# Reordering the first stage of a fused four-layer kernel: lower products one cycle later, upper weights turned at once, another place for the rotary side jobs

## What is computed

```python
# per batch e of 4: x[e] is 512 x 512, guw = fside_sq[e] (512 x 512), dw = ctx[e] (512 x 256)
def smooth_quant_linear(x, w):
    s = sqrt(max(amax(|x|, axis=0), EPS) / max(amax(|w|, axis=0), EPS))     # one factor a column
    xs, ws = x / s, w * s
    x_scale, w_scale = rowmax(|xs|) / 127, rowmax(|ws|) / 127
    return round(xs / x_scale) @ round(ws / w_scale).T * x_scale * w_scale.T

def expert(xe, guw, dw):
    gate, up = split(smooth_quant_linear(xe, guw), 2)                       # the "upper" linear
    return smooth_quant_linear(silu(gate) * up, dw)                         # the "lower" linear

x = x + tanh(g_xattn[0]) * expert(layernorm(x), fside_sq, ctx)              # layer 1: this stage
x = x + tanh(g_ffn[0])   * moe(layernorm(x), ...)
x = x + tanh(g_xattn[1]) * attention(layernorm(x), ctx, rotary positions, ...)
x = x + tanh(g_ffn[1])   * moe(layernorm(x), ...)
```

## Time and profile before

| | us |
|---|---|
| three runs, median | 1309.74 |
| lowest, highest | 1307.85, 1311.29 |
| profiled execution | 1311.2 |
| its span | 1309.5 |
| first stage: last write to X | 217.85 from the span's start |
| next stage: first transfer issued | 222.35 |

### The profile page before, as it was taken

One profiled execution on the slowest core, in us unless ns is written; L12 is line 12 of the kernel. 1 busy time (PEld: TensorE's weight loads), 2 busy tenths in 40 slices (PEclk: granted clock), 3 DMA queues, 4 the chain that ended last, 5 costly groups with the idle time before them and its releaser, 6 DMA issues.

```text
span 1309.5 us, 16528 instructions
## 1 busy us (share of the span) xinstructions
PE 1169.4 (89%) x5292; PEld 508.2 (39%) x5293; DVE 831.5 (63%) x1292; ACT 661.6 (51%) x1157; POOL 398.6 (30%) x465
## 2 busy tenths in 40 slices
PE   5877776998999999968889989999999999889997
PEld 4554442555444444423222223222322222234543
DVE  6788665335455554155878888778877777724543
ACT  2665564465222222244466666566656656763453
POOL 4456541102322222042234432222222233102332
PEclk8988898999999999988999999999999999999999
DMA  7334124654544444188314443222222225300011
GB/s 244 126 105 137 49 97 159 226 211 161 192 146 156 149 148 135 54 255 196 90 48 139 128 126 94 79 77 83 75 82 82 79 81 61 50 1 9 33 41 49
DMA packets 111893, 145.79 MB, mean 111 GB/s; under 512 B 25048, under 2 KB 79832, under 8 KB 111560
## 3 DMA queue, kind: packets, MB, share of 16 engines
q1 hardware_dynamic: 92680, 113.47, 27.2%
q0 software_dynamic: 18368, 28.85, 8.6%
q10 hardware_dynamic: 768, 2.49, 0.6%
HBM read 99.54 MB, written 48.37 MB: 113 GB/s over the span
## 4 chain that ended last, share of the span: by engine, by line
PE 33%; DVE 10%; issue 7%; ACT 5%; POOL 1%; DMA 1%; ACTq 0%; POOLq 0%; DVEq 0%
PE PS L2902 7%; PE PS L2803 5%; PE PS L2868 5%; PE PS L2887 4%; DVE a_top L3263 4%; PE PS L2827 3%; PE PS L2387 2%; ACT shared_w L3023 2%; ACT a_E L3023 2%; PE PS L2410 1%; PE PS L1980 1%; PE PS L2014 1%; POOL a_K L2147 1%; DMA a_rows<-f_y,l_pos 1%; PE PS L2815 0%
## 5 line engine op out<-in xcount | busy, mean ns | idle before, releaser
L3263 DVE TENSOR_REDUCE a_top<-PS 128x2 f32<-128x1024 f32 x256 | 309.3, 1222 | 88.4 <-PE PS L2887 84.9
L2868 PE MATMUL PS<-a_Q,a_K 99*128 99x512 bf16 (+1 forms) x512 | 166.2, 386 | 15.1 <-ACT a_E L3023 3.2
L3023 ACT ACTIVATE shared_w<-PS 128x512 f32<-128x512 f32 x256 | 138.8, 596 | 74.7 <-PE PS L2868 74.6
L3023 ACT ACTIVATE a_E<-PS 128x512 f32<-128x512 f32 x256 | 138.9, 596 | 63.7 <-PE PS L2868 63.5
L1498 PE MATMUL PS<-f_W,f_GT 128*128 x312 | 142.2, 599 | 0.2 <-ACT f_GT L1532 0.2
L2887 PE MATMUL PS<-a_K,a_Q 64*128 64x512 bf16 x512 | 100.5, 390 | 7.9 <-DVE a_top L3263 6.4
L1927 POOL TENSOR_TENSOR a_qf<-a_qf,a_tab 128x512 f32<-128x512 f32 x15 | 19.1, 1270 | 286.4 <-DVE a_swapped L3165 286.4
L2868 PEld LDWEIGHTS PS<-a_Q,a_K 99*128 99x128 bf16 (+1 forms) x512 | 44.1, 97 | 150.1 <-ACT a_E L3023 51.1
L1554 DVE TENSOR_TENSOR f_H<-f_SG,PS 128x256 f32<-128x256 f32 x39 | 16.4, 421 | 115.5 <-ACT f_SG L1538 115.5
L1498 PEld LDWEIGHTS PS<-f_W,f_GT 128*128 128x128 f32 x312 | 56.9, 192 | 57.9 <-issue 57.9
L2803 PE MATMUL PS<-a_xT,a_early 128*128 128x512 f32 x128 | 72.9, 667 | 2.0 <-ACT a_xT L2989 0.7
(11 more groups left out here) (382 smaller groups left out, 2076.8 us busy)
## 6 DMA issues: line engine op xcount, KB each, us to landing
f0r_raw<-in_L_ffn_W_dram SPq DMA_DIRECT2D x24, 512.0 KB, 5.3
a_K<-k_parts SPq DMA_DIRECT2D x192, 64.0 KB, 2.3
a_Q<-a_q_parts SPq DMA_DIRECT2D x186, 64.0 KB, 2.4
f_y<-f_Y SPq DMA_DIRECT2D x39, 256.0 KB, 2.0
v_units<-V SPq DMA_DIRECT2D x16, 512.0 KB, 2.9
a_V<-v_units SPq DMA_DIRECT2D x16, 512.0 KB, 3.6
k_parts<-f_k_parts SPq DMA_DIRECT2D x16, 384.0 KB, 3.4
a_q_parts<-a_parts SPq DMA_DIRECT2D x16, 384.0 KB, 2.8
```

Source lines behind the costliest of these rows:

```text
L2868: nc.tensor.matmul(PS[:, 4 + h % 2, :], K6[k][0:rows_, o, head // 2, kt * P:(kt + 1) * P], Q6[k][0:rows_, o, head // 2, :], start=True, st ...
L3023: nc.scalar.activation(E[step % 2][:, h, :], PS[:, 4 + h % 2, :], ACT.Exp).then_inc(exp_done, 1)
L3263: nc.vector.tensor_reduce(top[:, h - h % 2:h - h % 2 + 2, t], PS[:, 2 * pair:2 * pair + 2, :], AX.X, ALU.max).then_inc(maxed, 1)
```

## The change

The order on all four engines is rewritten; no arithmetic is changed. In cycle i there is now a third batch, `e = i - 2`: its lower products and their rescaling (y) go into the front of cycle i, in banks 4, 5, 6 and again 4, and POOL adds y of batch b - 2 in its pass b. PE turns the first half of the upper weights as soon as they are shifted and no longer behind the lower wsc_row; the upper products come before the turn of the lower xs. DVE has `gate` behind `s_columns(up)`, and the lower reductions later. ACT loads the root's table right behind silu (by `norm_root`, or by a spare Sqrt, `bring_root`), and makes the waves of batch i at the end of cycle i, ahead of slot 7; r of batches 1 to 3 stands in slot 7 of the cycle before, now in front of the slot's own job. The numbers of jobs in the slots stay.

```diff
-        DOWN_AT = (4, 5, 6, 0)
+        DOWN_AT = {b: (4, 5, 6, 4) for b in range(NB - 2)}
+        DOWN_AT[NB - 2] = (4, 5, 6, 2)
+        DOWN_AT[NB - 1] = (0, 1, 2, 5)
@@ POOL
             for b in range(NB):
                 side.pool_angles(pool, b)
-                if b:
-                    (adds y of batch b - 1)
+                if b >= 2:
+                    add_batch(b - 2)
+                if b == NB - 1:
+                    add_batch(NB - 2)
                 side.pool_tables(pool, b)
@@ PE, cycle i
                 turn_w(up, u, 1, 2)
-                if d >= 0: turn_w(down, d, 0, 4)
                 turn_w(up, u, 0, 0)
...
                 turn_x(up, u, 0, 0)
+                if e >= 0:
+                    pe.wait_ge(down.xqT_ready, e + 1)
+                    lower_products(e, (0, 1, 2))
                 side.tensor(pe, i, 1)
-                if d >= 0: turn_down_x(d)
+                if e >= 0:
+                    pe.wait_ge(y_ready, e * TB + 1)
+                    lower_products(e, (3,))
                 s_rows(up, u, (0, 0), (1, 0))
+                if d >= 0: turn_w(down, d, 0, 4)          # waits for y of batch e
                 side.tensor(pe, i, 2)
-                if d >= 0: s_rows(down, d, (6, 0), (6, 256))
+                if d >= 0: turn_down_x(d, 4)
                 side.tensor(pe, i, 3)
                 wsc_row(up, u, 1)
                 side.tensor(pe, i, 4)
+                pe.wait_ge(up.w_shifted, u + 1)
+                turn_shifted(up.ws, 0, (2, 3), up.wqT_done)
+                if d >= 0: s_rows(down, d, (6, 0), (6, 256))
                 side.tensor(pe, i, 5)
-                if d >= 0: wsc_row(down, d, 4)
-                finish_up(u)
-                side.tensor(pe, i, 6)
-                if d >= 0: finish_down(d)
+                (the rest of what finish_up was)
+                if d >= 0:
+                    wsc_row(down, d, 4)
+                    turn_down_ws(d)
                 pe.wait_ge(up.xqT_ready, 2 * u + 2)
                 for t in range(TB):
                     product(up, t, t)
-                if d >= 0: (lower products 0 to 2)
+                side.tensor(pe, i, 6)
+                if d >= 0: turn_down_xs(d)
                 side.tensor(pe, i, 7)
-                if d >= 0: (lower product 3)
@@ ACT, cycle i
                 if d >= 0:
-                    side.scalar(act, d, 7)
-                    side.scalar_waves(act, d)
                     silu(d)
+                    if u < NB - 1: norm_root(u + 1)
+                    else: bring_root()
                 side.scalar(act, i, 0)
-                side.scalar(act, i, 1)
                 root(up, u)
-                if d >= 0:
-                    root(down, d)
-                    if u < NB - 1: norm_root(u + 1)
+                side.scalar(act, i, 1)
...
                 take_wsc_row(up, u, 1)
+                if d >= 0: root(down, d)
                 side.scalar(act, i, 4)
+                take_up_w(u, 0, 2)
                 shift_x(up, u)
...
+                take_up_w(u, 1, 0)
                 side.scalar(act, i, 5)
-                take_up_w(u)
                 if d >= 0:
                     shift_w(down, d)
                     take_wsc_row(down, d, 4)
-                    shift_x(down, d)
+                if 0 < u < NB - 1: normalize(u + 1)
+                if d >= 0:
+                    take_down_w(d)
+                    shift_x(down, d)
                 side.scalar(act, i, 6)
-                if d >= 0: take_down_w(d)
+                if u == 0: normalize(1)
+                if u < NB - 1:
+                    side.scalar_waves(act, u)
+                    side.scalar(act, i, 7)
                 if d >= 0: take_down_x(d)
-                if u < NB - 1: normalize(u + 1)
@@ ACT, tail
             d = NB - 1
+            silu(d)
+            bring_root()
             side.scalar(act, d, 7)
-            silu(d)
@@ DVE, cycle i: new order
+                reduce_turned(up) x4; ratio(up)
+                if e >= 0: take_down(e, (0, 1))
+                s_columns(up)
+                if e >= 0: take_down(e, (2,))
+                if u == 1: row_stats(3)
+                if d >= 0: gate(d)
+                if e >= 0: take_down(e, (3,))
+                scale_w(up); reduce_turned(down, d, 0); w_scales(up)
+                reduce_turned(down, d, 1); ratio(down)
+                scale_x(up); s_columns(down); x_scales(up); row_shifts(u + 1)
+                scale_w(down); w_scales(down); take_up_x(u)
+                scale_x(down); x_scales(down); gate_scale(d); take_up(u)
@@ SideJobs
-    ANGLES = 1
+    ANGLES = ((0, 1), (0, 7), (1, 7), (2, 7))
-                slots.append(flat[:many] + ([(i, "r", 0)] if s == self.ANGLES and i < self.NB else []))
+                slots.append([(b, "r", 0) for b in range(self.NB) if self.ANGLES[b] == (i, s)] + flat[:many])
```

More of the change, by code:

```diff
@@ L448, in normalize, with bring_root @@
                 last.then_inc(up.x_ready, 1)
+            def bring_root():
+                nc.scalar.activation(spare_root[:], ln_eps[:], ACT.Sqrt)
             norm_root(0)
@@ L602, in gate_scale, with take_down @@
                 ch.wait()
-            def take_down(b, last):
+            def take_down(b, tiles):
                 v.wait_ge(down.wsc_row_ready, b + 1)
@@ L607, in take_down @@
                     v.wait_ge(x_updated, b * TB)
-                for t in range(TB):
+                for t in tiles:
                     v.wait_ge(down.product_done, b * TB + t + 1)
-                    nc.vector.scalar_tensor_tensor(y[:, t, :], PS[:, (LAST_AT if last else DOWN_AT)[t], :], gated_scale[:, t:t + 1], down.wsc_row[:],
+                    nc.vector.scalar_tensor_tensor(y[:, t, :], PS[:, DOWN_AT[b][t], :], gated_scale[:, t:t + 1], down.wsc_row[:],
                                                    ALU.mult, ALU.mult).then_inc(y_ready, 1)
-                    if last and t:
-                        add_rows(b, t - 1)
-                if last:
-                    add_rows(b, TB - 1)
             def add_rows(b, t):
@@ L633, in _ @@
                 reduce_turned(up, u, 3, 0)
+                ratio(up, u)
+                if e >= 0:
+                    take_down(e, (0, 1))
+                s_columns(up, u)
+                if e >= 0:
+                    take_down(e, (2,))
+                if u == 1:
+                    row_stats(3)
                 if d >= 0:
                     gate(d)
-                ratio(up, u)
-                s_columns(up, u)
+                if e >= 0:
+                    take_down(e, (3,))
+                scale_w(up, u, 1, 0)
+                if d >= 0:
+                    reduce_turned(down, d, 0, 4)
+                w_scales(up, u)
                 if d >= 0:
@@ L640, in _ @@
                     ratio(down, d)
-                scale_w(up, u, 1, 0)
+                scale_x(up, u, 0, 0)
                 if d >= 0:
                     s_columns(down, d)
-                w_scales(up, u)
-                x_scales(up, u, 0, 0)
+                x_scales(up, u)
+                if 0 < u < NB - 1:
+                    row_shifts(u + 1)
                 if d >= 0:
@@ L649, in _ @@
                     w_scales(down, d)
-                    x_scales(down, d, 6, 0)
+                if u == 0:
+                    v.wait_ge(x_loaded[1], 16)
+                    row_stats(1)
+                take_up_x(u)
+                if u == 0:
+                    row_shifts(1)
+                if d >= 0:
+                    scale_x(down, d, 6, 0)
+                    x_scales(down, d)
                     if d == 0:
@@ L677, in _ @@
             w_scales(down, d)
-            x_scales(down, d, 6, 0)
+            scale_x(down, d, 6, 0)
+            x_scales(down, d)
             gate_scale(d)
-            take_down(d, True)
+            for t in range(TB):
+                take_down(d, (t,))
+                if t:
+                    add_rows(d, t - 1)
+            add_rows(d, TB - 1)
             v.wait_ge(x_updated, NB * TB)
```

145 lines of the change are left out of this document (63 added, 82 removed).

## The result

| | before | after |
|---|---|---|
| median of the runs, us | 1309.72 (with the runs made beside the kernel after) | 1326.19 (1325.49 to 1327.38) |
| span of the profiled execution | 1309.5 | 1324.7 |
| last write to X in the first stage | 217.85 | 230.42 |
| rest of the span | 1091.65 | 1094.3 |

What follows compares the result with a forecast made beforehand. DVE carries most of the first stage's chain, with holes for the root, hs and turned weights. A1 54.35, cycles 46.1 and 43.4, last cycle and tail 77.2 end it at 221.05 (+3.2): 1312.9 us, range 1303.5 to 1319.

Steps and rivals of the forecast that it cites:

- the new middle: Upper x_scaled to upper products, with ACT as the chain: 7.0 us, where it took 13.3 and 15.0 before.
- A1: End of the pass over batch 0, when PE starts turning batch 1's upper weights: 54.35, against 50.06 before.
- signs of being wrong: Gate at 1.4, small steps at 0.17, PE's side job behind ang at 1.9 each time, or A1 below 52.
- The new end of a cycle: Upper products to PE's next turn of upper weights, behind the wait for ang: 10.9 in cycle 1, 8.55 in cycle 2.
- the clock's 0.8: PE's side job after the wait for ang may run at the low clock: half of 1.7, 0.8 in cycle 1.
- the rival that it falls each time: PE's clock drops after every wait for ang: another 3.1 us, 1316.0; slower, by this or larger stalls, had 0.37.
- The front, with stalls beside POOL: Start of upper weight turns to x_scaled on DVE, stalls of 3.5 included: 27.4 in cycle 1, 27.0 in cycle 2.
- part 3: DVE's work from the start of upper weight turns to x_scaled, without stalls: 23.5 us, against 25.4 before.
- Last cycle, from the products on: Last upper products to stage end, V job behind silu and root table; last cycle and tail 77.2 against 75.3.
- Edits at nothing: add_batch on POOL, stores on SP's queue, the split of x_scales and spare_root (0.2) were taken to cost nothing.
- DVE runs through: Rival: small steps fall into POOL's gaps and PE's clock stays high: -6.2 us, 1303.6; chance 0.21.
- the even exchange: Rival: cycle ends give back what the middle gains, 1309.7; chance 0.42 together with no change and the forecast.

Runs made afterwards that it cites:

- tail_copies: Kernel after, with ACT in the tail copying slot 7's two V jobs before silu(3) and the root's table: ratio 1.0066 to the kernel before.
- no_angles_after: Kernel after, with POOL's reduction of the angles left out (rotary tables hold other numbers): ratio 1.0063 to the kernel before.
- own_jobs_later: Kernel after, with the jobs behind r in slot 7 of cycles 0 to 2 moved to slot 0 of the next cycle: ratio 1.0033 to the kernel before.
- tail_gate_first: r_own_tail, with gate ahead of every y in the tail: ratio 0.9897 to the kernel before, 1295.76 us.
- r_own_tail: Kernel after, with r back in its own cycle and, in the tail, ACT's slot 7 copies ahead of silu(3): ratio 0.9906 to the kernel before.

## Why the prediction was wrong, point by point

Against the forecast the end of the stage came 9.4 us late (230.42 for 221.05).

Three steps failed, all of them terms of the sum that were too small: the stalls beside POOL in the front of the cycles, gate above all (+7.3), the new middle (+3.5), and the part from the last upper products on, where gate stands beside POOL's additions (+3.9). A1 and the cycle ends, forecast too long, took back 5.4. Two of the forecast's own signs of being wrong came, A1 below 52 and a side job behind ang at about 1.9; both hang on the execution that was profiled, as the next lines tell.

- **A1** (forecast 54.35, measured 50.90, -3.4). The products ran 2.5 earlier than summed, of which 1.9 is the early turn of x in the first pass and not the change. The step itself, V job behind ang behind waves, came as told: PE's wait was 3.57, I had 3.8. With x turned late, the same code up to there gave 54.97 in tail_copies, so that the -3.4 is mostly the luck of this execution, in the forecast's favour: it hid a part of the miss.
- **The new end of a cycle**, from the products to the next A: 10.65 and 8.53. The working (10.9 and 8.55) was right to 0.3; the clock's 0.8 on top wasn't there, as the side jobs of four matmuls behind ang took 1.98 each. In tail_copies, with the same code, they took 3.64 and 2.50, in no_angles_after 1.98 and 3.40. So the level goes either way from one execution to the next, which is what a half of 1.7 meant; the rival that it falls each time is out.

```profile
51.49 3.64 PE L1851 MATMUL PS<-wkv,cT 128*128 128x512 f32 x4 [3.57 <-ACT ang L1871]
```

- **The new middle** (7.0): 7.8, 8.4 and 8.3, so +3.5 in three cycles. The step was mis-sized. PE waited 1.11, 0.77 and 0.77 for ACT's copy of the lower row in front of the lower turns, which stand ahead of the products, and in cycle 1 a side job at the clock's low level (3.62, at 77.84) ran into the chain.
- **The front, with stalls beside POOL** (27.4, 27.0, 27.0): 28.6, 29.1 and 31.0, +7.3 in all. This is the largest miss. I put 1.1 on gate, the size of one stall; it had 1.5, 2.6 and 2.4, which is 3.2 of the 7.3. Each of gate's four instructions can be held up, and I counted one. The small steps lost 8.3 in the three cycles where I had 7.2. The waits for copies and turned tiles inside the front, and the first turns of the last cycle at the clock's low level (3.09 for 1.91), are most of the rest. About 0.8 is an error of addition: the terms of part 3 add up to 23.85 and not 23.5, and with row_stats(3) in place of the y's, cycle 1 comes to 27.5. Behind gate stands the last y, for which PE waits before it turns the lower weights (4.24 and 4.08), a follower I had not named; DVE did not wait for it.
- **Last cycle, from the products on** (43.2): 47.1, +3.9. The V job was there (3.96 of wait, then 3.78 at the low level), and the turned weights came 15.3 us behind the products, where I had 14.3. From there to the end of the last reduction it took 11.55 instead of 8.8: gate 3.56 instead of 2.34, and 1.6 in the turns on both sides of it (1.91 for the weights' eight, 1.52 for those of a). What stretched gate are POOL's additions, which I had counted as one stall of 1.0 in the tail.
- **Edits at nothing.** The stores and spare_root held. add_batch did not: I only asked whether it would be late, not what it would run beside, and no_angles_after shows it beside gate in the cycles as well.
- **The rivals.** That DVE runs through is out; so is the even exchange, though it was nearest in kind: the middle gave 15.0 to 8.4, and the end, front and tail took it back and more. None of the rivals was about the last cycle and the tail, where 11 of the 12.6 us lie.
- **The moved r as a whole.** I priced it by its wait, 2 to 4 us at each end, and the waits came so. Undone, it gave 22.7 us, of which the stage has 21.8: 17.2 less of DVE's waits for PE, 6.1 less of gate, 1.4 more of waits for ACT. Without the angles the same step gives 20 us, 14.3 of them waits for PE. So the queue is the greater part and gate's place the smaller. own_jobs_later does not bear on this split, as its 9 us came off gate and the small steps; how much of the waits is PE's order, ACT's order or the clock is open.
- **The range** was built around stalls of up to 5 per cycle in the cycles alone; it had nothing for the last part, where three terms were short at once. Its low end has all terms at one end, its high end not; with all of them it would have been 1320.5, still below what was measured.

## What to carry to other kernels

A job that waits for a busy engine costs what stands behind it in the same queue: before moving it, list that, and ask whether the wait's present cover moves with it; here r moved with the waves cost nothing in sum on the old order, where the waves gave back what r took, and r alone 22.7 us on the new. A good change can be lost in what comes with it: the new middle alone gave 9.6 us, and the reordering around it lost that and 16.5 more. Ask of every operation that another engine starts by itself (additions behind y) not only when it is done but what it will run beside.

## What the runs showed of the hardware

- Gate's four two-input operations on SBUF can each be held up beside POOL. They took 0.41 to 0.42 each alone (1.42 together in the kernel before). In cycle 2 of the kernel after, beside the angles, they took 0.42, 1.49, 0.84 and 1.50 (4.00 together), and in its tail, beside three additions of 4.09 together, 0.42, 1.49, 1.48 and 0.41 (3.56 together). The Trainium skill (SBUF — State Buffer, section "SBUF: two separate sides") calls the shared port an exclusive lock for a whole instruction; the trace agrees in kind, as no single one was held up by more than 1.1, which is less than the POOL operation beside it (1.26 to 1.41). For a forecast, count the instructions that can be held up, not the groups: three of four were in cycle 2, two of four in the tail.
- The first pass has two courses that don't go with the kernel: the turns of xh took 3.18 (late) or 1.91 (early), and the second upper reduction started at 17.83 or 15.92. Here they are, from the kernel before and the kernel after. The kernel after was early and tail_copies, with the same code up to there, late. The granted clock in the rows from 14 to 18 us is 1.00 in both, so it does not name the cause, which is open. A difference of 2 us between two profiled executions can be that alone; with the level of the side job behind ang, A1 differs by 4.1 (50.90 and 54.97).

```profile
15.81 3.18 PE L263 MATMUL PS<-identf,xh 128*128 128x128 f32 x16
```

```profile
14.77 1.91 PE L271 MATMUL PS<-identf,xh 128*128 128x128 f32 x16
```

- Leaving the angles out moved the granted clock from 50 to 200 us from 0.91 to 0.98 in the kernel before, and not at all in the kernel after (0.88 both times), where PE's waits for ang remained. So part of the angles' 10.5 us may have been clock; the runs don't part the two. The same holds for tail_gate_first, which had 0.98 there and r_own_tail 0.93.
